# Units of 320 columns in tile 4, the sums transposed a slot earlier, and the scatter directly behind its root

## The reference

```python
q_blhd = jnp.einsum('bld,dhk->blhk', x_bld, Wq)
latent_bll = jnp.einsum('bld,dc->blc', x_bld, Wkv_down)
attn = softmax(where(mask, q . k / sqrt(64), neg_inf));  y = attn . v;  out = y . Wout
x = layernorm(x + out)
top1 = argmax(softmax(xt @ w_router));  slot = top1 * C + pos, if pos < C   # C = 320
y = (silu(buf @ w_gate) * (buf @ w_up)) @ w_down
x = layernorm(xt + y[slot] * gate)
```

## Time and profile before

| | us |
|---|---|
| three runs | 2629.75, 2627.61, 2628.47; median 2628.47 |
| profiled execution, own time | 2634.99 |
| its span, first to last instruction | 2632.9 |
| busy PE | 2370.9 (90%) |
| busy DVE, ACT, POOL | 1658.6 (63%), 1030.6 (39%), 1680.8 (64%) |
| mean granted PE clock | 0.961 |

### The profile page before, as it was taken

One profiled execution on the slowest core, in us unless ns is written; L12 is line 12 of the kernel. 1 busy time (PEld: TensorE's weight loads), 2 busy tenths in 40 slices (PEclk: granted clock), 3 DMA queues, 4 the chain that ended last, 5 costly groups with the idle time before them and its releaser, 6 DMA issues.

```text
span 2632.9 us, 36668 instructions
## 1 busy us (share of the span) xinstructions
PE 2370.9 (90%) x11528; PEld 1518.4 (58%) x11528; DVE 1658.6 (63%) x4490; ACT 1030.6 (39%) x1992; POOL 1680.8 (64%) x1623
## 2 busy tenths in 40 slices
PE   6999999989998999899999999899989999868985
PEld 5555565556655665566555655566556655546663
DVE  4677656766677667666776577656766677334443
ACT  3444434443444335433444244433443344112222
POOL 1687656865686668765786568666876578413333
PEclk8999998999999999999999989999999999969998
DMA  2222100200011001100110002000110011134551
GB/s 83 60 64 72 37 15 15 66 16 13 17 52 30 17 13 41 41 17 13 25 57 17 13 13 69 13 17 13 49 37 13 13 38 31 62 107 136 167 168 65
DMA packets 96816, 118.95 MB, mean 45 GB/s; under 512 B 12288, under 2 KB 75782, under 8 KB 96624
## 3 DMA queue, kind: packets, MB, share of 16 engines
q1 hardware_dynamic: 89712, 99.98, 13.8%
q0 software_dynamic: 6912, 16.64, 1.8%
HBM read 46.91 MB, written 37.90 MB: 32 GB/s over the span
## 4 chain that ended last, share of the span: by engine, by line
PE 46%; POOL 25%; issue 15%; DVE 7%; ACT 2%; DMA 1%; POOLq 0%; SPq 0%; DVEq 0%; ACTq 0%
POOL half_sums L500 12%; PE value_ps L720 9%; PE turned_ps L697 6%; PE misc_ps L742 6%; PE turned_ps L700 5%; PE misc_ps L619 5%; POOL half_sums L495 4%; PE turned_ps L889 4%; PE row_ps L672 3%; POOL probs L475 3%; PE misc_ps L732 3%; POOL headsT L507 2%; POOL slots_x L532 2%; DVE unit_max L1118 2%; PE turned_ps L672 1%
## 5 line engine op out<-in xcount | busy, mean ns | idle before, releaser
L962 ACT ACTIVATE probs<-turned_ps 128x512 f32<-128x512 f32 (+2 forms) x1280 | 652.4, 553 | 800.5 <-PE turned_ps L700 785.5
L500 POOL TENSOR_TENSOR half_sums<-half_sums,probs 128x1024 f32<-128x1024 f32 (+3 forms) x512 | 829.7, 1621 | 56.1 <-ACT probs L962 41.8
L720 PE MATMUL value_ps<-probs,lat_keys 128*64 128x512 f32 (+3 forms) x3072 | 607.3, 511 | 68.8 <-POOL probs L475 64.3
L697 PE MATMUL turned_ps<-q_hl,lat_hi 128*128 128x512 f32 (+2 forms) x1280 | 536.0, 419 | 1.7 <-ACT fold_v L1007 1.7
L475 POOL TENSOR_SCALAR_AFFINE_SELECT probs<-probs 128x256 f32<-128x256 f32 x512 | 211.6, 413 | 466.9 <-ACT probs L962 465.9
L1114 DVE CUSTOM_DVE_ANT_0 masked_row<-row_ps,future 128x128 bf16<-128x128 f32 (+3 forms) x707 | 333.8, 492 | 264.0 <-PE row_ps L672 258.3
L700 PE MATMUL turned_ps<-q_max,lat_lo 65*128 65x512 f32 (+2 forms) x1280 | 486.5, 380 | 2.8 <-DMA q_max<-both_rows 2.8
L720 PEld LDWEIGHTS value_ps<-probs,lat_keys 128*64 128x64 f32 x3072 | 184.3, 138 | 373.3 <-issue 187.9
L495 POOL TENSOR_TENSOR half_sums<-probs 128x768 f32<-128x768 f32 (+1 forms) x128 | 268.9, 2101 | 140.9 <-ACT probs L962 140.9
L697 PEld LDWEIGHTS turned_ps<-q_hl,lat_hi 128*128 128x128 f32 x1280 | 246.9, 193 | 164.6 <-issue 98.5
L672 PE MATMUL row_ps<-lat_hi,q_hl 128*128 128x512 f32 (+3 forms) x1026 | 320.1, 352 | 18.8 <-DVE unit_max L1114 10.1
(11 more groups left out here) (192 smaller groups left out, 2700.2 us busy)
## 6 DMA issues: line engine op xcount, KB each, us to landing
q_max<-q_hl SPq DMA_DIRECT2D x256, 128.0 KB
slots_x<-router SPq DMA_DIRECT2D x8, 1290.0 KB, 6.1
ex_x<-slots_x SPq DMA_DIRECT2D x64, 129.0 KB, 3.6
x_in<-in_L_attn_x_bld SPq DMA_DIRECT2D x8, 1024.0 KB, 5.6
layer_out<-x_in SPq DMA_DIRECT2D x8, 1024.0 KB, 4.5
ex_w<-in_L_ffn_w_gate SPq DMA_DIRECT2D x32, 256.0 KB, 3.7
ex_w<-in_L_ffn_w_up SPq DMA_DIRECT2D x32, 256.0 KB, 3.7
ex_w<-in_L_ffn_w_down SPq DMA_DIRECT2D x32, 256.0 KB, 4.0
```

The source lines that it names most:

```text
L500: nc.gpsimd.tensor_tensor(total, total, now[:, :, q0:BANK], ALU.add).then_inc(added, 1)
L697: nc.tensor.matmul(scores_of(n, h), lat_hi[b % 2][:, keys], q_hl[gp % 2][:, heads, cols], start=True, stop=False)
L720: mm = nc.tensor.matmul(value_ps[h * LD:(h + 1) * LD, q0:BANK], lat_keys[b % 2][:, j, :], probs[:, n % NPROBS, h, q0:BANK], start=(j == 0) ...
L962: nc.scalar.activation(probs[:, n % NPROBS, heads, q0:BANK], scores_of(n, h), ACT.Exp).then_inc(exp_done, 1)
```

## The change

Four things change. (1) Tile 4's four units per pair have 320 columns each, keys 0 to 319 and 320 to 639; the mask now belongs to the second, and its last 128 columns are the masked ones. (2) DVE transposes the sums at the end of its own slot 4, no longer in slot 5. (3) On DVE the uses of `LATE[gp, t]` come ahead of `invert_rows` in slots 6 and 8. (4) In the tail POOL sends group g back directly behind root(g), ACT normalises group g - 1 after the first expert of group g and no longer after the second, and SP loads rows ahead of weights from the ninth expert on.

```diff
--- before.py
+++ after.py
@@ -53,6 +53,9 @@
     UNITS = ([(h, i, 0) for i in range(HPB) for h in range(2)]
              + [(h, i, k) for i in range(HPB, NT) for k in range(2) for h in range(2)])
     NU = len(UNITS)
+
+    unit_keys = lambda i, k: ((k * 5 * P // 2, (k + 1) * 5 * P // 2) if i == HPB
+                              else (k * BANK, min((i + 1) * P, (k + 1) * BANK)))
 
     UNITS_AT = {(gp, t): [(gp + 1, u) for u in range(2 * t, 2 * t + 2)] for gp in range(PAIRS - 1) for t in range(NSLOT)}
     for t in range(HPB):
@@ -430,8 +433,8 @@
             for e in range(AHEAD, E):
                 g = (e - AHEAD) // 2
                 sp.wait_ge(ex_sent[g % 2], 16 * NY * (g // 2 + 1))
+                load_rows(e)
                 load_weights(e)
-                load_rows(e)
             for k in range(2):
                 sp.wait_ge(ex_sent[k], 16 * NY * (E // 4))
 
@@ -582,9 +585,7 @@
 
             for g in range(E // 2):
                 root(g)
-                if g:
-                    send_back(g - 1)
-            send_back(E // 2 - 1)
+                send_back(g)
 
         @block.tensor
         def _(pe):
@@ -667,7 +668,7 @@
                 if n >= 2:
                     if n in ROW_BEFORE:
                         pe.wait_ge(max_done, ROW_BEFORE[n] + 1)
-                k0, k1 = k * BANK, min((i + 1) * P, (k + 1) * BANK)
+                k0, k1 = unit_keys(i, k)
                 dst = ROW_BANKS[row_bank(n)]
                 nc.tensor.matmul(dst[:, 0:k1 - k0], q_hl[gp % 2][:, h, i * P:(i + 1) * P], lat_hi[b % 2][:, k0:k1],
                                  start=True, stop=True).then_inc(rows_full, 1)
@@ -1046,8 +1047,8 @@
             for e in range(0, E, 2):
                 for u in range(2):
                     activate(e + u)
-                if e:
-                    normalise_out(e // 2 - 1)
+                    if e and u == 0:
+                        normalise_out(e // 2 - 1)
             normalise_out(E // 2 - 1)
 
         @block.vector
@@ -1101,7 +1102,8 @@
                 h, i, k = UNITS[u]
                 n = UNIT[gp, u]
                 c = i // HPB
-                width = min((i + 1) * P, (k + 1) * BANK) - k * BANK
+                k0, k1 = unit_keys(i, k)
+                width = k1 - k0
                 at = h * HPB + i % HPB
                 if u in (0, 2 * HPB) and gp:
                     dve.wait_ge(misc_full, MISC["maxT", gp - 1, c] + 1)
@@ -1110,7 +1112,7 @@
                 row = ROW_BANKS[row_bank(n)]
                 if n >= 2:
                     dve.wait_ge(max_done, n - 1)
-                if k * BANK + width == (i + 1) * P:
+                if k1 == (i + 1) * P:
                     nc.vector.tensor_tensor_reduce(masked_row[n % 2][:, 0:width], row[:, 0:width], future[:, BANK - width:],
                                                    scale=-1.0, scalar=-MASKED, op0=ALU.add, op1=ALU.min, accum_out=dst
                                                    ).then_inc(max_done, 1)
@@ -1288,13 +1290,11 @@
                         for use in LATE[divmod(gp * NSLOT + t - 1, NSLOT)]:
                             if use[0] == "q":
                                 low_q(*use[1:])
-                            if use[0] == "sums":
-                                invert(*use[1:])
+                    for use in LATE[gp, t]:
+                        if use[0] in STAGES and use[0] != "q":
+                            STAGES[use[0]](*use[1:])
                     if gp and t in (6, 8):
                         invert_rows(gp - 1, t // 8)
-                    for use in LATE[gp, t]:
-                        if use[0] in STAGES and use[0] not in ("q", "sums"):
-                            STAGES[use[0]](*use[1:])
                     if b and (p, t) in ((1, 5), (2, 0)):
                         variance(b - 1, p - 1)
                     if b and (p, t) in ((1, 10), (2, 4)):
```

## The result

| | before | after |
|---|---|---|
| median of four runs, us | 2628.52 (2627.61 to 2629.75) | 2605.97 (2603.41 to 2607.56) |
| span of the profiled execution | 2632.9 | 2603.4 |
| attention, first slot to start of the tail's first gate matmul | 53.5 to 2341.7 | 53.3 to 2348.0 |
| first to last group of the tail (sixteen) | 249.1 | 221.0 |
| last group to the end | 42.1 | 34.4 |

A forecast was written before the change was run, and what follows sets the result against it. TensorE, busy 90% of the span, was taken to bound the kernel through its stops. Terms -35.3 - 17.6 - 6.3 + 34.2 - 5 - 26 - 8.3 = -64.3 gave 2570.7, 2564 against the median; forecast 2565 us, range 2542 to 2594.

The forecast's parts named there:

- both_rows in slot 7: Attention slot 7: PE's 0.84 us wait for both_rows, written behind slot 6's inversion, goes in 21 pairs: -17.6 us.
- xT in p = 6, slot 9: Low half of xT moves before the second inversion in slot 8, shortening PE's 1.25 us wait: -0.9 us, 7 times, -6.3.
- new stop in slot 8, plain pairs: Slot 6's copies meet a GpSimd addition, so PE stops 1.15 us in slot 8 of 20 pairs: +23 us, bounds 0 to 48.
- slot 8 of p = 3, 7, 2 and 6: Smaller stops in pairs with something in slot 7: +4.9 us for p = 3, +3.5 for 7, +2.8 for 2 and 6.
- clock besides: Half-clock stretches behind slot 5's stop in p = 7 partly go, new stops bring others: -5 us, bounds -11 and +20.
- tail, groups: Tail: scatters some 12 us earlier release loads sooner, 13 groups approach 14.65 us each: -26 us, bounds 0 and 28.
- maxT before the inversion: Slots 6 and 8: LATE uses run before the inversion; gains of 17.6 and 6.3 us against a loss of 34.2 us.
- Rival C: Inversion meets additions in slots 6 and 8, half clock behind: 4.2 us per pair over 62, about 2795 us; chance 0.04.
- Rival A: No new stop in slot 8, because the copies find a gap between GpSimd's additions: 2531 us; chance 0.11.
- Rivals B: Tail stays bound by its loads, DMA needing 10 us per two experts; only the end gains: 2591; 0.14 shared with D.
- E: The change does not do what it says, loads and scatters wait for something else: within 0.2%, about 5 us; chance 0.03.
- D: Attention gains nothing on balance, only the tail does (34.3 us): 2594 us; chance 0.14 shared with Rivals B.

The follow-up runs named there:

- the kernel before with reductions: The kernel before, with only the two 32 x 16 copies of each inversion written as tensor_reduce over a size-1 axis: 2611.86 us, ratio 0.9931.
- the reductions: The changed kernel with nothing moved, the two 32 x 16 copies of each inversion written as tensor_reduce over a size-1 axis: 2526.64 us, ratio 0.9598.

## Why the prediction was wrong

Against the terms of its sum:

| term | predicted | shown by the slots |
|---|---|---|
| widths | 0 | 0 by the medians (2607.9 against 2606.0), -7 by the slots |
| sums in slot 4 | -35.3 | -1.26, -1.91, -1.21, -1.07 in 28 pairs, -38; alone -1.19 to -1.34, -36 |
| both_rows in slot 7 | -17.6 | -0.93, -0.70, -0.88 in 21 pairs, -17.6 |
| xT in p = 6, slot 9 | -6.3 | -5.7 |
| new stop in slot 8, plain pairs | +23 | +23.2 (p = 4 8.9, p = 5 6.7, six others 1.26 each) |
| slot 8 of p = 3, 7, 2 and 6 | +11.2 | +4.6, +2.9, +5.5 |
| second inversion, p = 3 slots 9, 10 and p = 6 slot 10 | 0 | +28 and +15 |
| clock besides | -5 | p = 7 slot 6 -11, p = 5 slots 4 and 5 +11; p = 2 slots 4 and 6 -6, p = 3 slots 0 and 1 +4 |
| tail, groups | -26 | -28.1 |
| end | -8.3 | -7.7 |

The rows on slots are from the two traces and give the 6.6 us that the attention lost to within 3 us; the rest is slot 4 of p = 4 and roundings.

**The step that failed** is "The change part by part", maxT before the inversion. The prediction followed the copies of slot 6 in detail, price and place both right, and stopped there. It took the second inversion, in slot 8, as unmoved: for p = 3 it counted "0.7 us by DVE's longer queue", and for p = 6 it booked only the gain of the same move. But the delay of slot 8 is handed on: in p = 3 the copies had 0.29 us of room before the next addition, and the 0.8 us that DVE handed on took that. It had the means: the rule of the lock, and the trace of both places. Some 43 us went there, 28 of them in seven pairs, where slot 10 lost 3.6 to 4.0 us in the four that had run at full clock there and 2.4 to 2.5 in the three that had not; with them the forecast would have been about 2608. Rival C named this mechanism (a second meeting, with the clock behind it) and gave it to all 62 pairs with a chance of 0.04; it came true in fourteen, and its counterargument, that PE does not stop for the second meeting, held in all pairs but those.

A second point was right in its number and wrong in its reason. The waits for both_rows and for xT_lo were put down to the order of DVE's queue; the kernel before with reductions shows that they were the copies' wait for the addition. Part (3) moved a held instruction behind its victim instead of freeing it, so it could only change who waits. Rival A (no new stop, 2531) is what the reductions gave, 2526.6, by a way that the prediction had not thought of. Rivals B and E fell with the tail; B's 10 us of DMA work per two experts stands in no row, and after the change the DMA engines are busy for 0.57 of the 14.65 us of a group, 8.4 us. D is 12 us off in time (2594) and not right in kind, since in the attention pairs that gained 62 us and pairs that lost 69 met. That the forecast missed by 41 us and not more is in part luck: p = 2 gave 10 us more than its terms, with less time at half clock, which its clock term did not name.

The clock: p = 7 came as predicted (9 us named, 11 found), the stretches it expected behind new stops came in p = 3, and those of p = 5 in slots 4 and 5 it had no reason for. Over the pairs of batches 1 to 7, time at half clock went from 34.5 to 7.5 us in p = 2, from 23.6 to 70.2 in p = 3, from 0 to 23.9 in p = 5 and from 20.5 to 0 in p = 7. Why p = 5 has them in the change is not settled: part (1) and the held copies both move them (slots 4 to 6: +1.6 us per pair in the change, +1.4 with its part (1) undone, +1.2 with reductions, 0 with both), but no run shows what sets one off.

## What to carry to other kernels

Where two engines exclude each other, an instruction moved in a queue written by hand has to be followed through every later meeting with the other engine until the delay has died out, not only through the one beside its new place; a margin of 0.3 us between a copy and the other engine's next instruction belongs into the sum as a term. Before moving an instruction whose duration varies (here 0.16 to 2.3 us for one shape), look at what it overlaps when it is long, and first try a form of it that can't be held: that was worth 79 us in the changed kernel and 18 in the kernel before, and the move 38 us the wrong way. Parts of a change are to be priced together where they touch one queue: alone the four gave +20, -40, +64 and -32 us, +12 in sum, and together -22.5.

## What the runs showed of the hardware

- A copy of 32 x 16 fp32 values takes 0.16 us alone and waits for the whole rest of an addition of GpSimd on 128 x 1024 values, up to 2.34 us; a reduction of the same values takes 0.16 us always, though 215 of 256 run beside an addition.
- Not only copies are held: an addition of two bf16 tiles in SBUF (L1240) took 2.22 us beside POOL's addition and, with the copies as reductions, 0.42 us where it began 0.06 us ahead of one; L1243 (two inputs of 128 x 8) took 2.28 us beside one and 0.17 us without. The subtraction that makes xT_lo, one of whose inputs is in PSUM, took 0.65 to 0.69 us everywhere, the reciprocal 0.21 to 0.26, though 118 of its 128 began inside an instruction of POOL.
- Kernels whose matmuls are nearly the same and whose stops of PE, of about 1 to 3 us, fall in other places spend different times at half clock in the attention: 54.6, 61.4, 85.3, 95.6, 116.1 and 170.7 us in six of these. What sets a stretch off no run here shows. A change of 0.2 us in two maxima (the widths) was worth 0, 10 or 20 us, by what else stood in the queue; of the 20, some 16 are longer waits and not the clock.
